# The token choice between two transformer layers: constants built in the first batch, 16-bit views, two parallel place counts, and lists moved by TensorE

## The reference, cut to what matters

```python
n_tokens, n_experts, capacity = 8192, 16, 512
xn = xf / rms * norm_weight
logits = xn @ router_weight.T + router_bias          # 8192 x 16
probs = softmax(logits, axis=-1)
_, idx = top_k(logits.T, capacity)                   # 16 lists of 512 tokens
xe = xn[idx]
h = gelu(einsum('ecd,efd->ecf', xe, fc1_weight) + fc1_bias)
y = einsum('ecf,edf->ecd', h, fc2_weight) + fc2_bias
gates = take_along_axis(probs.T, idx, axis=1)
output = zeros.at[idx].add(y * gates)                # over all experts
gate_sums = zeros.at[idx].add(gates)
output = where(gate_sums > 0, output / gate_sums, output)
```

## Time and profile before

| | us |
|---|---|
| median of 3 runs (lowest, highest) | 1809.23 (1808.62, 1812.13) |
| the profiled execution's own time | 1809.41 |
| its span in the profile | 1807.4 |
| batches | 0 to 1448 |
| selection, to the first gather | 1448 to 1591 |
| experts | 1591 to 1807.4 |
| busy over the span: PE, DVE, ACT, POOL | 84%, 66%, 48%, 30% |

### The profile page before, as it was taken

The page is one execution under the profiler, slowest core; times in us unless marked ns, Lnnn a source line. Parts: engine busy times, 40 slices in busy tenths (PEclk is TensorE's granted clock), DMA queues, the critical chain, the costliest instruction groups (busy, mean ns, idle before and its releaser), DMA issues.

```text
span 1807.4 us, 33637 instructions
## 1 busy us (share of the span) xinstructions
PE 1509.6 (84%) x10072; PEld 920.9 (51%) x10072; DVE 1187.1 (66%) x3463; ACT 859.7 (48%) x1787; POOL 546.6 (30%) x626
## 2 busy tenths in 40 slices
PE   2879999999999999999999999999988711447674
PEld 1445656565655556565656565655644311435563
DVE  5477778686878787777868687878756278801110
ACT  0426464646465555646464646555552522423331
POOL 1323222232313132323222231313130120058886
PEclk8879999999999999999999999999997855678888
DMA  2030221213030303031121303030302000044443
GB/s 73 1 82 25 65 55 42 63 32 86 9 88 7 87 16 85 27 68 51 44 57 38 83 13 88 7 87 16 79 26 65 17 2 1 7 93 81 98 84 60
DMA packets 83238, 90.70 MB, mean 50 GB/s; under 512 B 19520, under 2 KB 73024, under 8 KB 78528
## 3 DMA queue, kind: packets, MB, share of 16 engines
q1 hardware_dynamic: 71872, 80.76, 18.0%
q0 software_dynamic: 11264, 8.92, 3.6%
HBM read 58.95 MB, written 29.92 MB: 49 GB/s over the span
## 4 chain that ended last, share of the span: by engine, by line
PE 54%; DVE 17%; issue 12%; POOL 7%; DMA 3%; ACT 3%; SPq 1%; DVEq 1%; POOLq 0%; ACTq 0%
PE fa L702 7%; PE ba L608 6%; PE ba L603 6%; PE fa L694 6%; PE bo L861 6%; PE ba L614 5%; PE fa L712 4%; POOL out L573 3%; PE facc L712 2%; DVE passed L1496 2%; POOL got L543 2%; DVE nm L1286 2%; DMA QT<-nmT 2%; PE ba L981 1%; PE bo L770 1%
## 5 line engine op out<-in xcount | busy, mean ns | idle before, releaser
L1041 ACT ACTIVATE probs<-ba 128x512 f32<-128x512 f32 x640 | 349.6, 599 | 131.7 <-PE ba L614 129.5
L458 POOL TENSOR_TENSOR x<-x,gd 128x512 f32<-128x512 f32 x144 | 182.6, 1268 | 589.8 <-ACT gd L1019 573.3
L603 PE MATMUL ba<-QT,KT 75*128 75x512 bf16 (+3 forms) x1024 | 233.4, 306 | 26.1 <-ACT probs L1041 13.4
L608 PE MATMUL ba<-KT,QT 72*128 72x512 bf16 (+3 forms) x1024 | 230.4, 305 | 7.6 <-DVE nm L1289 3.2
L1286 DVE TENSOR_REDUCE nm<-ba 128x1 f32<-128x512 f32 x256 | 174.4, 681 | 34.2 <-PE ba L614 34.0
L861 PE MATMUL bo<-probs,vp 128*32 128x512 f32 (+3 forms) x2048 | 181.8, 444 | 2.0 <-ACT probs L1041 0.9
L603 PEld LDWEIGHTS ba<-QT,KT 75*128 75x128 bf16 x1024 | 87.5, 100 | 174.4 <-ACT probs L1041 103.4
L702 PE MATMUL fa<-f_nT,w 128*128 128x512 f32 x320 | 170.3, 614 | 3.4 <-DVE hh L1278 3.1
L694 PE MATMUL fa<-f_nT,w 128*128 128x512 f32 x320 | 169.6, 612 | 0.0
L614 PE MATMUL ba<-mask_q,identb 128*128 128x256 bf16 (+1 forms) x640 | 163.8, 256 | 0.0
L614 PE MATMUL ba<-mask_k,identb 128*128 128x256 bf16 (+1 forms) x640 | 163.5, 255 | 0.0
(11 more groups left out here) (279 smaller groups left out, 2668.1 us busy)
## 6 DMA issues: line engine op xcount, KB each, us to landing
QT<-qk_parts SPq DMA_DIRECT2D x96, 192.0 KB
KT<-qk_parts SPq DMA_DIRECT2D x96, 192.0 KB
qk_parts<-qkp SPq DMA_DIRECT2D x32, 384.0 KB, 2.6
fc<-in_L_ffn_fc_weight SPq DMA_DIRECT2D x32, 256.0 KB
xin<-in_L_attn_x SPq DMA_DIRECT2D x16, 256.0 KB, 7.4
qk_parts<-qkp SPq DMA_DIRECT2D x16, 256.0 KB, 2.7
out<-x SPq DMA_DIRECT2D x16, 256.0 KB, 2.3
xn_rows<-row SPq DMA_DIRECT2D x16, 256.0 KB, 7.2
```

Of the source, the lines that this page charges most:

```text
L458: pool.tensor_tensor(x1[:], x1[:], gd[:, e % 2], ALU.add).then_inc(S["s_x1g"], 1)
L603: pe.matmul(bank[:, col:col + w], lhsT=KT[0:K_ROWS, head, blk * P:(blk + 1) * P], rhs=QT[0:K_ROWS, head, blk * P:], start=first_, stop=False)
L608: pe.matmul(bank[:, col:col + w], lhsT=QT[0:QK_ROWS, head, blk * P:(blk + 1) * P], rhs=KT[0:QK_ROWS, head, 0:w], start=first_, stop=False)
L1041: act.activation(probs[:, pair % 3, f_], ba[n % 3][:], ACT.Exp, scale=SCALE).then_inc(S["s_exp"], 1)
```

## The change

It has four parts.

**Constants.** All constants but `ones` and `tile_of` are built by a new function `choice_constants`, which POOL calls once, at the end of phase Y of batch 0. A new 128 x 128 pattern `quad`, ones in blocks of 4 x 4 on the diagonal, is among them.

**16-bit views.** `high16` and the low half are no longer made by four instructions: they are strided views of the 32-bit `keys`. The low search runs on float32 `low` itself, `low16` is gone. The slots are written as int16 (`slot16`, `low4`, `hi`), and `hot_hi` compares int16 `hi` with 16 h where it compared float16 with h. `picked` is one instruction over an unsigned view of `slot16` where it was two over PSUM.

**Places in parallel.** The counts of the chosen above the threshold and of those equal to it are summed by two products behind one wait. The equal ones get the places behind all that are above, by an own scan. What falls at 512 or beyond is dropped later, since no one-hot tile matches it. The two place tiles are turned and added by PE in 2 x 8 accumulating f32 products with `ident`, in place of 8 transposes of one tile.

**Lists by TensorE.** `idx` is f32. DVE spreads it by `own4` into 4 x 64 columns, one PE product with `quad` copies it within each group of 4 partitions, and DVE masks and reduces to `idx_pc`. The DRAM tensor and its 5 DMAs are gone.

The diff, cut to its core:

```diff
+            def choice_constants():
+
+                for m in range(1 - GJ, GJ):
...
+                    const(pool.affine_select(same_e[:], same_e[:], [[-1, P]], ALU.not_equal, 1.0, base=E1 * m, channel_multiplier=1))
+                    if m > 0:
+                        const(pool.affine_select(earlier_e[:], earlier_e[:], [[-1, P]], ALU.not_equal, 1.0, base=E1 * m, channel_multiplier=1))
+                const(pool.memset(quad[:], 1.0))
+                const(pool.affine_select(quad[:], quad[:], [[-4, P // 4], [0, 4]], ALU.is_ge, 0.0, base=0, channel_multiplier=1))
+                const(pool.affine_select(quad[:], quad[:], [[4, P // 4], [0, 4]], ALU.is_ge, 0.0, base=3, channel_multiplier=-1))
...
                     power(f_rs[:, 0:Q], f_ve[:, 0:Q], "s_varf", "s_rsf", 2 * f + 2)
+                if isinstance(f, int) and f == 0:
+                    choice_constants()
...
             pool.memset(ones[:], 1.0).then_inc(S["s_ec"], 1)
...
             pool.tensor_copy(tile_of[:], tcol[:, :, :, None].to_broadcast([P, 8, GJ, E1])).then_inc(S["s_ec"], 1)
...
             sp.wait_ge(S["s_idx"], 1)
-            for e in range(4):
-                sp.dma_start(lists.rearrange("(q e) (h l) -> e h q l", e=4, l=16)[e], idx[e:P:4]).then_inc(S["s_ldw"], 16)
-
             sp.dma_start(fb1[:], a["L1_ffn_fc1_bias"]).then_inc(S["s_fb"], 16)
-            sp.wait_ge(S["s_ldw"], 64)
-            sp.dma_start(idx_pc[:], lists.rearrange("e (p c) -> p e c", c=CC)).then_inc(S["s_ldr"], 16)
...
-            across(0, same_e, cnt, "s_gtc", 1, "s_gtt")
-            across(0, earlier_e, cnt, "s_gtc", 2, "s_gtt")
-            across(0, earlier_e, cnt, "s_gtc", 3, "s_gtt")
-            pe.wait_ge(S["s_rc"], 1)
-            for g in range(8):
-                last = pe.transpose(fa[g // 4][:, (g % 4) * P:(g % 4 + 1) * P], place[:, g * P:(g + 1) * P], ident[:])
+            across(0, earlier_e, cnt2, "s_gtc", 1, "s_gtt")
+            across(2, same_e, cnt2[:, 0:1], "s_gtc", 1, "s_gtt")
+            for k, part in enumerate((above_at, equal_at)):
+                pe.wait_ge(S["s_rc"], k + 1)
+                for g in range(8):
+                    last = pe.matmul(fa[g // 4][:, (g % 4) * P:(g % 4 + 1) * P], lhsT=part[:, g * P:(g + 1) * P], rhs=ident[:],
+                                     start=k == 0 and g % 4 == 0, stop=k == 1 and g % 4 == 3)
             last.then_inc(S["s_slT"], 1)
...
+            pe.wait_ge(S["s_idx"], 2)
+            pe.matmul(fa[2][:, 0:256], lhsT=quad[:].rearrange("p h l -> p (h l)"), rhs=idx_own[:].rearrange("p q e l -> p (q e l)"),
+                      start=True, stop=True).then_inc(S["s_quad"], 1)
...
-            ks(dve.tensor_scalar(half_i[:], keys[:], 16, None, ALU.arith_shift_right))
-            ks(dve.tensor_copy(high16[:], half_i[:]))
-            ks(dve.tensor_scalar(half_i[:], keys[:], 2 ** 16 - 1, None, ALU.bitwise_and))
-            ks(dve.tensor_copy(low[:], half_i[:]))
+            high16 = keys[:].bitcast(I16).rearrange("p (w t) -> p w t", t=2)[:, :, 1]
+            unsigned_low = keys[:].bitcast(U16).rearrange("p (w t) -> p w t", t=2)[:, :, 0]
...
-            ls_(dve.scalar_tensor_tensor(low[:], high16[:], found_high[:], low[:], ALU.is_equal, ALU.mult))
-            ls_(dve.tensor_scalar(low16[:], low[:], -2.0 ** 15, None, ALU.add))
+            ls_(dve.scalar_tensor_tensor(low[:], high16, found_high[:], unsigned_low, ALU.is_equal, ALU.mult))
...
-            digits(8, low16, found_low)
+            digits(8, low[:], found_low)
...
-            ec(dve.tensor_copy(thr_hi[:], found_high[:]))
-            ec(dve.tensor_scalar(found_low[:], found_low[:], 2.0 ** 15, None, ALU.add))
+            ec(dve.tensor_copy(thr_hi[:], found_high[:]), False)
...
+            dve.tensor_scalar(above_t[:], LT[:], thr, None, ALU.is_gt, ALU.add, accum_out=cnt2[:, 0:1])
+            dve.tensor_scalar(equal_t[:], LT[:], thr, None, ALU.is_equal, ALU.add, accum_out=cnt2[:, 1:2]).then_inc(S["s_gtc"], 1)
             dve.wait_ge(S["s_gtt"], 2)
...
+            ec(dve.tensor_copy(offs[:, 0:3], fa[2][:, 0:3]))
+            ec(dve.tensor_tensor(offs[:, 3:4], offs[:, 1:2], offs[:, 2:3], ALU.add), False)
+            ec(dve.tensor_tensor_scan(above_at[:], ones[:], above_t[:], offs[:, 0:1], ALU.mult, ALU.add))
+            dve.tensor_tensor(above_at[:], above_at[:], above_t[:], ALU.mult).then_inc(S["s_rc"], 1)
+            ec(dve.tensor_tensor_scan(equal_at[:], ones[:], equal_t[:], offs[:, 3:4], ALU.mult, ALU.add))
+            dve.tensor_tensor(equal_at[:], equal_at[:], equal_t[:], ALU.mult).then_inc(S["s_rc"], 1)
             dve.wait_ge(S["s_slT"], 1)
...
+                sl(dve.tensor_scalar(slot16[:, half * 512:(half + 1) * 512], fa[half][:], -1.0, None, ALU.add), half == 1)
+            sl(dve.tensor_scalar(low4[:], slot16[:], 15, None, ALU.bitwise_and))
+            dve.scalar_tensor_tensor(ramp[:, 1], low4[:], float(TILES), tile_of[:].rearrange("p g j e -> p (g j e)"), ALU.mult, ALU.add)\
                .then_inc(S["s_ramp"], 1)
...
+            sl(dve.tensor_scalar(hi[:], slot16[:], -16, None, ALU.bitwise_and), False)
+            sl(dve.tensor_scalar(ramp[:, 0], low4[:], float(P), pcol[:], ALU.mult, ALU.add))
...
-                    dve.tensor_scalar(hot_hi[:, n, h], his, float(h), None, ALU.is_equal)
+                    dve.tensor_scalar(hot_hi[:, n, h], his, float(16 * h), None, ALU.is_equal)
...
+            gs(dve.tensor_scalar(picked[:].rearrange("p g j e -> p (g j e)"), slot16[:].bitcast(U16), CAP - 0.5, None, ALU.is_lt))
...
+            dve.wait_ge(S["s_idx"], 1)
+            dve.tensor_tensor(idx_own[:], idx[:, :, None, :].to_broadcast([P, 4, 4, 16]), own4[:, None, :, None].to_broadcast([P, 4, 4, 16]), ALU.mult)\
+               .then_inc(S["s_idx"], 1)
+            dve.wait_ge(S["s_quad"], 1)
+            dve.tensor_tensor(idx_quad[:], fa[2][:, 0:256].rearrange("p (x l c) -> p x c l", l=4, c=CC),
+                              own4[:, None, None, :].to_broadcast([P, E1, CC, 4]), ALU.mult).then_inc(S["s_lists"], 1)
+            dve.wait_ge(S["s_lists"], 1)
+            dve.tensor_reduce(idx_pc[:], idx_quad[:], X, ALU.add).then_inc(S["s_lists"], 1)
```

135 lines of the change are left out of this document (58 added, 77 removed).

## The result

The changed kernel takes 1791.64 us (median of 4 runs, 1791.54 to 1794.42) against 1808.92 for the kernel before (median of 4, 1808.16 to 1812.13). The ratio is 0.9902, with a 95% interval from 0.9887 to 0.9918: faster by 17.3 us, or 1%. The forecast was 1792.2. The profiled execution took 1791.54 us, its span is 1789.8.

A forecast was written before the change was run, and what follows sets the result against it. DVE bounds the selection and POOL the fixed-length experts, so an earlier first gather is the gain: 4.05 + 3.2 + 1.2 + 1.4 + 2.1 + 5.05 - 0.05 = 17.0 us off, forecast 1792.2, range 1789 to 1797.

The forecast's parts named there:

- Step 1: Start of the selection: with constants built early, DVE no longer waits 4.15 us for POOL; 4.05 us off.
- Steps 2 and 3: Keys and search: four splitting instructions fall away, 3.2 us; fewer instructions in the search, counts unchanged at 1.28, 1.2 us.
- Step 4: Equal count to slots: parallel places, PE's clock rising during the last 11 passes; 1.4 us off, bounds 0.1 and 2.
- Step 5: Making the slots after the places: 3.69 us instead of 5.78, with int16 at the rate of `hot_hi`; 2.1 us off.
- The one-hot tiles: 64 comparisons in `hot_hi` stay at 0.206 us each with int16 in; no gain or loss.
- slow int16: Rival in `hot_hi`: comparisons at half the rate, 1800.7 us (chance 0.05), or one element a cycle, 1817 (chance 0.04).
- half rate: Rival in the search: the strided view reads at half rate, adding 19.3 us, 1811.5; chance 0.03.
- Step 6: `idx` to first gather: without DRAM the gates' write decides, landing at 1585.3, gather 1.0 later; 5.05 us off.
- the rival in which `cur` decides: At the first gather: the gates' write is faster without list DMAs, first gather at 1584.9, total 1790.8; chance 0.04.

The follow-up runs named there:

- ones_late: The changed kernel with POOL writing `ones` only after DVE has its first candidates; 1789.75 us in one run.
- constants_back: The changed kernel with the call of `choice_constants` moved back behind the batches; 1795.68 us, 0.9916 of the kernel before.
- after: The changed kernel itself, with all four parts, against the kernel before; 1791.64 us, ratio 0.9902.
- best: The changed kernel with `ones_late`, `warm_long`, second-half tiles handed over in two parts and gates divided in each expert; 1796.01 us, 0.9929 of before.
- lists_back: The changed kernel with the lists written to DRAM and read back by 5 DMAs again; 1795.23 us.
- warm_long: The changed kernel with 34 unread PE products behind the product with `quad` and four more behind the first transposes; 1793.99 us.
- places_back: The changed kernel with the old places again, scans one after the other and 8 transposes of one tile; 1793.81 us in one run.

## Why the prediction was right, and where its terms were off

The two steps with the largest misses cancel, and in one of them the way that decided was not the one forecast. That the total lies within a microsecond is in part luck.

By its steps, in us gained from logits to first gather (17.03 in all):

| step | forecast | measured | |
|---|---|---|---|
| 1 constants | 4.05 | 3.31 | `half_i` 9.33 behind the logits before, 6.02 after |
| 2 splits | 3.2 | 3.26 | 5.39 to 2.13 |
| 3 search | 1.2 | 1.24 | B |
| 4 places | 1.4 | 1.31 | C |
| 5 slots | 2.1 | 1.79 | 5.78 to 3.99 |
| one-hot tiles to `idx` | 0 | -0.15 | 29.16 to 29.31 |
| 6 lists | 5.05 | 6.27 | D |

**Step 1** was the right mechanism with a mis-sized term: "a POOL memset beside DVE's first copy could hold that copy: 0 to 0.95 us, of which I take none, since DVE is released first". It held it by 0.83, near the upper bound, and `ones_late` shows that this is the cause. The reason that I gave was wrong in itself: DVE did start first, by 0.03 us (1448.02 and 1448.05), and it was DVE that took longer, while the memset kept its 0.95. The Trainium skill, SBUF — State Buffer, section "SBUF: two separate sides", says that the one that starts first has the shared ports for its whole instruction and the other blocks. By that rule, with the starts as the profile has them, the copy would have stayed at 0.69; the row differs, and it decides. What the rows do fit is one waiting for the whole of the other: the copy ended 0.54 us behind the memset (1449.54 and 1449.00), `half_i` of `constants_back` 0.55 (1458.74 and 1458.19), and the cast behind the memset took 0.45 longer in its turn. Only who was first can't be told from starts 0.03 us apart.

The moved block fits the first batch, 1.8 us ahead of the first addition to `x1`:

```profile
58.17 1.27 POOL L458 TENSOR_TENSOR x<-x,gd 128x512 f32<-128x512 f32 x1 [1.84 <-ACT gd L1029]
```

The four centring instructions of DVE, for which I took 0.05 us, were not held (1.12 us with and without the block). But small DVE instructions behind them were (`gt`, L1274, x2: 0.60 us, before 0.48). From the start of that stretch (38.82, before 39.02) to this addition it is 19.35 us against 18.91 before, and this is so throughout: 18.9 in the two kernels with the block behind the batches, 19.4 in all twelve with it in front. I had nothing for that. The whole of the batches doesn't show it (1408.5 to 1409.3 us against 1409.2, see `constants_back`).

**Steps 2 and 3** were sized right. The strided view costs nothing for counts at 1.28 us.

**Step 4** came out right in the profiled execution. The low rate was right (16 passes in 3.78 us, forecast 3.84), and the clock rose within the second group, as I had placed it, though after some 10 of its passes and not 5. In seven other kernels it rose sooner and the step gave 2.4; I had 2 as its upper bound. Of the twelve kernels with this chain only `after` and `best` have so late a rise, so that this term fits is in part luck.

**Step 5** was 0.3 too high. `low4` took 0.53 us from its start to the next instruction's, `hi` 0.33 and `ramp` 0 0.59, where I had 0.45, 0.26 and 0.45. I had worked from 0.206 us, the distance between comparisons that follow each other freely. One alone lasts longer: three take 0.72, which is two distances and 0.31. An instruction whose result is waited for costs its full duration and 0.1 more here (`low4` 0.43 and 0.10, `ramp` 0 0.48 and 0.11); `hi`, which isn't waited for, costs 0.33 of its 0.42.

**The one-hot tiles** kept 0.206 us. The rivals of slow int16 and of half rate are refuted. The 0.15 lost lies in the products: in the kernels with the earlier rise, tiles to `idx` take 29.15 us, and in `after` the products end 0.15 later behind the slots (31.03 against 30.88).

**Step 6** gave 1.2 more than forecast, and its statement "POOL's first gather needs both, and follows the landing by 1.0 as it followed `cur`" is what failed. The write landed in 7.5 us and not 8.4, and where it decides the gather follows it by 0.3 and not 1.0. That makes the way of the write 1.6 us shorter than I had it, so that in `after` the list came last: the product of 256 columns took 1.22 us, `cur` came 3 us behind `idx`, and the gather 1.17 behind `cur`. This is the rival in which `cur` decides, to which I gave a chance of 0.04; it had a gain of 6.5 (1591.36 - 1584.9), and 6.27 came. In the six kernels in which that product ran at the full clock the gates' write does bind, by 0.2 to 0.4 us. Undoing the lists alone cost 4.3 to 4.7 and not 6.3. The likely reason is that their way through DRAM also got shorter when the gates' write landed sooner; that is argued from two traces (`lists_back`), not shown.

The misses cancel: steps 1, 5 and the tiles gave 1.2 less (0.74, 0.31 and 0.15), step 6 1.2 more. That is why the total fits better than its terms.

## What to carry to other kernels

When two ways end at one point within a fraction of a microsecond, as the list and the gates' write do here, price both before shortening one, and find out which decides by the distance that each usually has to what it releases, not by the name in the bracket alone. Price the smaller pieces too: DVE instructions of half the size cost two thirds of the whole. When constants are moved out of a critical stretch, look at what stays of them, which large instruction it will run beside, and what the moved block will run beside where it goes. Put work for the clock's sake only where the engine waits, and count the gain in the stretch where the result is needed and not in the group that got shorter. As long as the late semaphore of `warm_long` is unexplained, look behind such work for a semaphore that comes late.

## What the runs showed that I had not expected

- A POOL memset of 1,024 float32 columns lengthens DVE's copy of the same size from 0.69 to 1.52 us, though the copy's recorded start is 0.03 us ahead. `half_i` grew from 0.69 to 1.41 beside the same memset, and a DVE instruction with two inputs from 1.23 to 1.86 beside POOL's cast. A reduction beside the cast (1.20) and the counts beside both (1.28) kept their time.
- The 512 KB write of the gates, in runs of 64 bytes, took 7.5 us to land in eight of the traces, 7.6 to 7.9 in four, 8.4 in the kernel before and 8.8 in `places_back`. A first gather that waits for it follows the landing by 0.3 us, one that waits for `cur` follows that by 1.17.
- The clock's rise within the same 32 passes comes at a different time in each execution (the second group took 2.05 to 3.11 us with nothing changed ahead of it), and that alone moves the end by 1 us.
- Unread products ahead of and behind the first transposes go with a delay of 3.4 to 4.2 us in the semaphore of the transposes.
